# Two self-attentions of a perceiver kernel: all row maxima taken beside the projections over four PSUM banks, low halves subtracted on TensorE, the values' projection after the others

## The reference, cut to what matters

```python
# first self-attention ("s0" in the kernel): causal
att = jnp.einsum('bhqd,bhkd->bhqk', q, k) * scale
att = jnp.where(causal[None, None] == 0, big_neg, att)
att = jax.nn.softmax(att, axis=-1)
x = jnp.einsum('bhqk,bhkd->bhqd', att, v)
...
# second self-attention ("s1"): centred heads, and a product of variances
qc = q - q.mean(axis=-1, keepdims=True)
kc = k - k.mean(axis=-1, keepdims=True)
cov = jnp.einsum('bhsd,bhtd->bhst', qc, kc) / D
var_comp = q_var[..., :, None] * k_var[..., None, :] / D
attn = jax.nn.softmax(cov + var_comp, axis=-1)
out = jnp.einsum('bhst,bhtd->bhsd', attn, v)
```

## Time and profile before

| what | value |
|---|---|
| median of 3 runs | 1817.34 us (1812.93 to 1818.72) |
| profiled execution, its own time | 1811.63 us |
| its span in the trace | 1809.9 us |
| mean granted clock | 0.927 |
| PE busy | 1580.1 us (87%) |
| DVE busy | 1163.3 us (64%) |
| ACT busy | 867.6 us (48%) |
| POOL busy | 684.6 us (38%) |

### The profile page before, as it was taken

How to read it: one execution, slowest core, us unless ns; L and a number is a source line. 1 busy time by engine, 2 the same in 40 slices (tenths; PEclk the granted TensorE clock), 3 DMA queues, 4 the chain that set the end, 5 groups by cost and what they waited for, 6 DMA issues and landing times. The chain is left out here.

```text
span 1809.9 us, 42047 instructions
## 1 busy us (share of the span) xinstructions
PE 1580.1 (87%) x15948; PEld 891.9 (49%) x15948; DVE 1163.3 (64%) x1757; ACT 867.6 (48%) x1162; POOL 684.6 (38%) x525
## 2 busy tenths in 40 slices
PE   3999999999499999997775958999999999966772
PEld 1455545554133333334342425777777777752432
DVE  4665656565599999993328647666666666335356
ACT  2555555555177777774220014555555555512330
POOL 2340000000111111111423007999999999917100
PEclk9999999999599999998777978999999999978786
DMA  4697888878332222220300047565556555021000
GB/s 164 193 217 239 208 233 212 239 210 213 108 95 64 67 64 69 63 64 9 143 1 1 1 122 223 137 162 149 148 134 164 147 150 130 11 83 38 2 0 12
DMA packets 178219, 212.19 MB, mean 117 GB/s; under 512 B 57096, under 2 KB 151572, under 8 KB 173486
## 3 DMA queue, kind: packets, MB, share of 16 engines
q1 hardware_dynamic: 177520, 210.45, 42.6%
q10 hardware_dynamic: 576, 0.00, 0.0%
HBM read 122.78 MB, written 87.57 MB: 116 GB/s over the span
## 5 line engine op out<-in xcount | busy, mean ns | idle before, releaser
L1121 POOL TENSOR_TENSOR x_r<-x_p 128x1024 f16<-128x1024 f32 x256 | 479.3, 1895 | 23.3 <-ACT x_p L1097 16.6
L1136 DVE TENSOR_REDUCE x_mx<-a_all 128x2 f32<-128x1024 f32 x249 | 304.9, 1225 | 147.3 <-PE a_all L1020 147.3
L1097 ACT ACTIVATE x_p<-s_all 128x1024 f32<-128x1024 f32 x256 | 248.4, 1022 | 222.7 <-PE s_all L1003 222.7
L702 ACT ACTIVATE x_p<-s_all 128x1024 f32<-128x1024 f32 x256 | 261.0, 1023 | 48.7 <-PE s_all L612 41.4
L757 DVE TENSOR_REDUCE x_mx<-a_all 128x1 f32<-128x512 f32 x352 | 229.8, 683 | 15.8 <-PE o_all L623 8.7
L1003 PE MATMUL s_all<-x_q,x_k 64*128 64x256 f16 x3072 | 209.5, 269 | 0.0
L1038 PEld LDWEIGHTS o_all<-x_v,x_p 128*128 128x128 bf16 x2048 | 178.7, 97 | 40.2 <-issue 40.1
L1038 PE MATMUL o_all<-x_v,x_p 128*128 128x129 f16 x2048 | 197.5, 221 | 0.9 <-POOL x_r L1121 0.9
L1039 PE MATMUL o_all<-x_v,x_r 128*128 128x65 f16 x2048 | 192.7, 193 | 0.0
L1039 PEld LDWEIGHTS o_all<-x_v,x_r 128*128 128x128 f16 x2048 | 180.7, 98 | 0.0
L1003 PEld LDWEIGHTS s_all<-x_q,x_k 64*128 64x128 f16 x3072 | 149.1, 94 | 61.9 <-issue 0.6
(11 more groups left out here) (343 smaller groups left out, 2829.3 us busy)
## 6 DMA issues: line engine op xcount, KB each, us to landing
values<-vst SPq DMA_DIRECT2D x16, 2064.0 KB, 10.2
x_v<-values SPq DMA_DIRECT2D x32, 1032.0 KB, 5.3
keys<-kst SPq DMA_DIRECT2D x32, 1024.0 KB, 6.6
x_k<-keys SPq DMA_DIRECT2D x128, 256.0 KB, 5.2
x_k<-keys SPq DMA_DIRECT2D x192, 64.0 KB, 2.1
values<-vst SPq DMA_DIRECT2D x16, 528.0 KB, 11.8
x_v<-values SPq DMA_DIRECT2D x32, 264.0 KB, 2.6
cf<-in_ctxT SPq DMA_DIRECT2D x16, 512.0 KB, 9.4
```

The lines of the kernel that those rows point to most:

```text
L702: act.activation(prob[g % NP][:], chip.s_ps[g % 2][:].rearrange("p (c q) -> p c q", q=SQ), ACT.Exp, scale=hd ** -0.5).then_inc(p_ready, 1)
L1097: act.activation(prob[g % NP][:], chip.s_ps[g % 2][:].rearrange("p (c q) -> p c q", q=SQ), ACT.Exp, scale=hd ** -0.5).then_inc(p_ready, 1)
L1121: pool.tensor_tensor(rest[g % NP][:], prob[g % NP][:], hi, ALU.subtract).then_inc(rest_done, 1)
L1136: dve.tensor_reduce(mx[a[1] % 2][:, n // 4, 2 * (n % 4):2 * (n % 4) + 2], chunk_banks(u, g)[:, :].rearrange("p (h c) -> p h c", h=2), AX.X ...
```

## The change

All sixteen tiles of coarse scores (now eight `row_scores(a)`, each with both tiles of 128 queries, a = batch + 2 * group) move into the projection part. Each fills the four banks of `s_all`, and each `maxima(a)` reduces all of it: in s0 in two instructions, over 512 and 1024 columns, in s1 in one over 2048. There is one `turn` over all four tiles of tokens, and one copy of 512 columns for it on ACT. The attention steps keep `scores`, `values` and `turned_output` and nothing else. The low half is no longer a subtraction on DVE: PE adds the product of a negated identity (`ident_neg`) with `hi` to the bank (`remainder(n)`), and ACT copies the bank (`low(n)`). `remainder` stands between the two matmuls of a later projection. The values' projection (`values_of(t)`) comes after the others, one tile between two `row_scores`, in the banks of `o_all`. PE's waits for the mask and for both identities now stand ahead of the first projection. In s1 DVE's `scales(0)` follows `maxima(1)`, and `scales(1)` and `scales(2)` follow the last maxima. Only the order, banks and engines change; the sum of what is computed is the same.

```diff
...
-                def project(n):
+                def project(n, k):
                     x, g = n % 2, n // 2
-                    if n >= 4:
+                    if n >= 4 and k == 0:
                         pe.wait_ge(lo_done, n - 3)
...
+                def remainder(n):
+                    pe.wait_ge(hi_done, n + 1)
+                    pe.matmul(pbank[n % 4][:], ident_neg[:], hi[n % 2][:, n // 2, :], start=False, stop=True,
+                              skip_group_check=True).then_inc(negated, 1)
+
                 def row_scores(a):
...
+                    b, g = a % B, a // B
+                    pe.wait_ge(hi_done, 2 * g + 2)
+                    if a >= 1:
+                        pe.wait_ge(nm_done, a)
+                    for t in range(2):
+                        n = P if mask is not None and t == 0 else SQ
                         for j in range(4):
                             r = slice(32 * j, 32 * j + 32)
...
+                def values_of(t):
+                    if t < 2:
+                        pe.wait_ge(lo_done, NQK - 3 + t)
                     else:
...
+                        pe.wait_ge(v_done, t - 1)
+                    for k in range(KT):
+                        last = pe.matmul(pbank[t % 2][:, 0:D], chip.xnT[:, k, t * P:(t + 1) * P], w[2][:, k, :],
+                                         start=(k == 0), stop=(k == KT - 1), skip_group_check=True)
+                    last.then_inc(v_ready, 1)
...
-                pe.wait_ge(weights[2].loaded, 16)
-                for t in range(NT):
-                    for k in range(KT):
-                        last = pe.matmul(chip.s_banks[t][:, 0:D], chip.xnT[:, k, t * P:(t + 1) * P], w[2][:, k, :],
-                                         start=(k == 0), stop=(k == KT - 1))
-                    last.then_inc(v_ready, 1)
                 pe.wait_ge(weights[0].loaded, 16)
                 pe.wait_ge(weights[1].loaded, 16)
                 pe.wait_ge(ld, 16)
...
+                pe.wait_ge(ident_made, 3)
+                if mask is not None:
+                    pe.wait_ge(mask_made, 2)
+                lag = 1 if spread is None else 2
+                for n in range(NQK + lag):
+                    for k in range(KT):
+                        if n < NQK:
+                            project(n, k)
+                        if k == 0 and spread is not None and 1 <= n <= NQK:
+                            variances(n - 1)
+                        if k == 0 and n >= lag:
+                            remainder(n - lag)
+                    if n - lag >= 1 and n < NQK:
+                        row_scores(n - lag - 1)
+                pe.wait_ge(weights[2].loaded, 16)
+                a = NQK - lag - 1
+                for t in range(NT):
+                    values_of(t)
+                    if a < NS:
+                        row_scores(a)
+                        a += 1
+                turn()
                 for i in range(NS):
                     scores(i)
-                    if i < NG:
-                        for t in range(2):
-                            row_scores(2 * NG + 2 * i + t)
-                    if i == NG - 1:
-                        turn(1)
                     if i >= 1:
                         values(i - 1)
...
+                def low(n):
+                    act.wait_ge(negated, n + 1)
+                    act.activation(lo[n % 2][:, n // 2, :], pbank[n % 4][:], ACT.Copy).then_inc(lo_done, 1)
...
-                def low(n):
-                    dve.wait_ge(hi_done, n + 1)
-                    dve.tensor_tensor(lo[n % 2][:, n // 2, :], pbank[n % 4][:], hi[n % 2][:, n // 2, :], ALU.subtract).then_inc(lo_done, 1)
...
-                for t in range(2):
-                    maxima(NQK - 2 + t)
+                for a in range(NS):
+                    maxima(a)
+                    if scales is not None and a == 1:
+                        scales(dve, 0)
                 for i in range(NS):
-                    if i < NG:
-                        for t in range(2):
-                            maxima(2 * NG + 2 * i + t)
+                    if scales is not None and i < 2:
+                        scales(dve, i + 1)
                     if i >= 2:
                         output(i - 2)
```

158 lines of the change are left out of this document (58 added, 100 removed).

## The result

| | before | after |
|---|---|---|
| median, same chip | 1815.21 us (4 runs) | 1785.22 us (4 runs, 1781.18 to 1787.54) |
| ratio | | 0.9831, 95% interval 0.9803 to 0.9858 |
| profiled execution, own time | 1811.63 us | 1787.54 us |
| its span | 1809.9 us | 1785.7 us |
| mean granted clock | 0.927 | 0.934 |

The kernel is 30 us faster; forecast were 26.3 (1791 us, with a range of 1781 to 1806). By the traces all of it lies in the two blocks. The first view is the timeline of the changed kernel's s0: where the block starts (DVE's cast), its first projection, a round, the turn, the first scores, and the next block.

A forecast was written before the change was run, and what follows sets the result against it. The prediction held the attention parts slow for the coarse scores' turn-taking between PE and DVE and for the 1.2 GHz clock. Its terms, 1.1 - 5.4 - 12.6 - 9.4 = -26.3 us, gave 1791 us from 1817.3, range 1781 to 1806.

The forecast's parts named there:

- The prediction's four terms: Projection part of s0 +1.1 us, projection part of s1 -5.4, attention part of s0 -12.6, attention part of s1 -9.4.
- three signs of being wrong: Granted clock in rounds 1 to 8 not 1.0; reductions over 2.0 and 2.4 us; PE waiting for ACT's low halves.
- 1.2 GHz for four steps, then, once the full steps run without a pause, 2.4 GHz: Attention parts of both blocks: likeliest course of the clock, giving s0 29.5 us (-12.6) and s1 33.8 us (-9.4).
- Rival 1: Attention parts: the clock never falls there, -35.3 us in sum, 1782 us; chance 0.12.
- rival 2: Attention parts: the clock stays at 1.2 GHz through both, -11.6 us in sum, 1806 us; chance 0.12.
- The projection part of s0: From s0's start to its first scores: first coarse scores at 866.4, seven rounds of 2.99 us, first scores at 891.5, +1.1 us.
- The chain that I named: Rounds of s0: scores to reduction 0.93 us, two reductions 1.92, back to PE 0.14; sum 2.99 us, which decides the round.
- The projection part of s1: From s1's start to its first scores: first coarse scores at 1638.3, PE's rounds 3.0 us, first scores at 1665.5, -5.4 us.
- The stall behind the scales: Projection rounds of s1: scales after maxima 1 hold DVE for 2.5 us, so PE stalls 1.75 us.
- Rival 3: End of s1: POOL's passes delay DVE's outputs and values 2, s1 loses about 6 us, 1797 us; chance 0.06.
- Rival 4: Projection rounds of both blocks: they lose the higher clock, +40 us, net +14, 1831 us; chance 0.04.
- Rival 5: Projection rounds: the turn-taking only moves, each of 16 costs 1.3 us more, about 1812 us, no difference; chance 0.04.

The follow-up runs named there:

- e6: Changed kernel with batch 1's coarse products again on PE in the first four attention steps, without DVE reductions or waits, results unused: 1794.71 us, ratio 0.9889.
- e4: Changed kernel with unread fp16 products of 512 columns in PE's last waits, around the turn and behind the first scores: 1786.80 us, ratio 0.9845.
- e3: Kernel before the change, same order, with unread fp16 products of 256 columns in PE's waits for DVE: 1802.15 us, ratio 0.9925.
- e5: Changed kernel with batch 1's coarse scores again in the first four attention steps, with DVE's reductions and PE's waits for them, results unused: 1809.61 us, ratio 0.9960.
- e1: Changed kernel with the low halves subtracted by DVE again, without PE's remainder product and ACT's second copy: 1781.74 us, ratio 0.9825 to before.
- e8: Changed kernel with PE's waits for mask and identities moved from the front to the first coarse scores and first remainder: 1786.95 us, ratio 0.9848.
- e11: Kernel of e8 with half of POOL's subtraction of the experts' weights in s0 moved, in six pieces, behind the masking of steps 1 to 6: 1783.05 us, ratio 0.9833.
- e9: Changed kernel with low halves on DVE, mask waited for late, two sets of scales ahead of maxima 0, PE's waits filled: 1777.30 us, ratio 0.9792.
- e10: Kernel of e9 with two more unread fp32 products of 512 columns at the front of s1: 1776.85 us, ratio 0.9802.

## Why the prediction was right, point by point

**The sum.** The prediction's four terms were +1.1, -5.4, -12.6 and -9.4 us; measured by the same marks they are +1.1, -3.0, -16.3 and -12.8, sum -31.0 for -26.3. The mechanism was right and the time fell inside the range; two terms were mis-sized in one way and one in the other, so part of the nearness of the sum is cancellation. None of the three signs of being wrong showed: the clock is 1.00 in the rounds, the reductions take 1.83 and 2.30 us, and PE never waits for ACT's low halves.

**The attention parts: the clock's share was over-priced.** The step that failed is "1.2 GHz for four steps, then, once the full steps run without a pause, 2.4 GHz". In s0 the steps began at 894.08, 896.72, 899.48, 902.70 and 905.34: four steps in 11.26 us for my 14.7, because only one of them was slow. In s1 three were:

```profile
1659.46 0.40 PE L1497 MATMUL s_all<-s_nmT,s_ident 32*128 32x256 f16 x4 [0.69 <-ACT s_nmT L1604]
...
1663.34 0.40 PE L1497 MATMUL s_all<-s_nmT,s_ident 32*128 32x256 f16 x4 [1.99 <-ACT s_p L1617]
...
1667.22 0.40 PE L1497 MATMUL s_all<-s_nmT,s_ident 32*128 32x256 f16 x4
...
1670.96 0.29 PE L1497 MATMUL s_all<-s_nmT,s_ident 32*128 32x256 f16 x4 [0.35 <-ACT s_p L1617]
```

The fourth took 3.04 us; four steps in 14.54 us for my 17.7: I had priced the third and fourth as full steps at 4.85 us, but the clock rose at 1668.7, 1.5 us into the third step, the first full one. That it rises where the waits for DVE are gone was foreseen; when it rises was a guess, and by e6 it is not told by PE's busy share alone. A step at 2.4 GHz was 2.64 and 3.04 us for my 2.73 and 3.13. Rival 1, "the clock never falls", is what s0 all but did (25.8 us for its 25.7) and what e4 shows to be possible; rival 2, low throughout, is far from every run with the new order.

**Which part of the gain is which.** Between first and last scores the blocks went from 71.9 to 42.8 us. By e3 the clock alone, in the old order, is 12.0. With the clock held nearly in the old order (0.93 and 0.95) and fully in the new, e3 against e4 (59.9 to 39.8), 20.1 are the coarse scores and their turn-taking. That most of this is the waiting for DVE is likely but not shown by itself: of the 24.2 us of e5, 16.5 are that waiting together with the lower clock that it brings. And 3.1 us (42.8 less 39.8) of the clock's price were still there after the change.

**The projection part of s0: right, by luck.** First scores were forecast 34.8 us after the start and came 34.8 after. But the first coarse scores came at +10.5 and not at +9.7, mostly since the clock rose 5.0 us after the first projection and not 3.7; the seven rounds took 2.91 us each and not 2.99; and from the last coarse scores to the first scores it was 3.9 us and not 4.2. The errors, +0.8, -0.6 and -0.3 us, cancel. The chain that I named does set the round: reduction 0.93 us after the scores, 1.83 us of reductions for my 1.92, 0.14 back. e1 confirms it: with the remainder gone from PE the round is still 2.91 us. PE waits for DVE only where a value tile is shorter than a projection, 0.94 and 1.09 us; in the earlier rounds PE and the chain are level, where I had 0.5 us of wait.

**The projection part of s1: +2.4 us over the forecast.** The rounds are PE's, as said, but 3.31 us long and not 3.0: I had taken 0.21 us for the coarse scores, which take 0.33, and the first fp32 product behind an fp16 group takes some 0.1 longer. The first coarse scores came 15.3 us after the start and not 13.6, and some 1.1 of these 1.7 us are the clock again (2.4 GHz at 1624.3, 6.0 us after the first projection for my 3.7); e1, with 2.8 us, shows that this is no fixed number. Behind the last projection PE also waits 0.36 and 0.47 us for ACT's squares and rounding, which makes one round of 3.75 us. The stall behind the scales was 0.70 us and not 1.75, because the longer rounds had left DVE 1 us of idle each. The reduction over four banks, 2.30 us, was forecast at 2.31.

**The rivals.** Rival 3, POOL's passes at the end of s1: they ended at 1686.0, 3.8 us ahead of the next block (1689.83), for a cover of 7 forecast. The mechanism was real, but its place was s0, where I had not looked: POOL's split of the experts' weights ended at 896.12, the first masking began at 896.16, and cover was nil (e8, e11). Rival 4, rounds that lose the higher clock: granted clock 1.00 in all of them. The Trainium skill's page "TensorE: Matmul & The Clock Gate", section "A second HAM failure mode: psum-queue depth-cycling", has the clock swing where matmul groups go round the banks with small idles between them; here PE was busy 21.31 of 24.20 us in s0's rounds and the clock did not swing; I had used the rule for rival 2's 1806 us, and the trace does not bear it out in the rounds. Rival 5, the turn-taking only moves: by e1 DVE has 0.5 us to spare in a round even with the subtraction.

**What I did not forecast.** That one of the three parts of the change works against it: the low halves on PE cost some 0.4 and 1.0 us (e1, with the clock's share taken off). My text asked only what the product costs, 0.21 us, and never whether DVE had the room, although its own numbers gave a round of 2.99 us with 1.92 of reductions in it.

## What to carry to other kernels

Where two engines take turns, gather what they exchange into fewer and larger hand-overs, in a part where the waiting engine has other work; here the wait that PE lost was paid back twice, since the clock no longer fell in it. Fill what wait is left, but look first at what comes due earlier in every queue that the waiting engine feeds or is fed by: three of the gains here (e8, e9, e10) ended at POOL's side job or at DVE's scales, and came back when these were cut or moved. And before work is moved from one engine to another, read the idle time of the first between its own chained operations: if it fits there, as DVE's subtraction did in e1, it is free where it is. Before an experiment's microsecond is put down to its edit, compare when the clock rose in both traces.
